# A macaron transformer block on one Trainium2 core: the low plane of the probabilities, made by GpSimd in its own slot or by VectorE one slot later

## The reference

```python
x = x + 0.5 * ffn(layernorm(x))      # gate, up: 256 -> 704, silu(gate)*up, down: 704 -> 256
x = x + attention(layernorm(x))      # causal, one head of width 256, 2048 keys a batch
x = x + 0.5 * ffn(layernorm(x))
```

```python
scores = Q @ K.T / sqrt(256); scores = where(causal, -inf, scores)
weights = softmax(scores);    out = weights @ V
```

## Time and profile before

| | |
|---|---|
| median of 3 runs | 1329.28 us |
| profiled execution, its own time | 1323.85 us |
| span of the profiled execution | 1322.0 us |
| PE busy | 1169.1 us (88%) |
| DVE busy | 1049.7 us (79%) |
| ACT busy | 732.5 us (55%) |
| POOL busy | 576.1 us (44%) |
| attention, as L549 runs | 473.8 to 920.0 us |

### The profile page before, as it was taken

One profiled execution on the slowest core, in us unless ns is written; L12 is line 12 of the kernel. 1 busy time (PEld: TensorE's weight loads), 2 busy tenths in 40 slices (PEclk: granted clock), 3 DMA queues, 4 the chain that ended last, 5 costly groups with the idle time before them and its releaser, 6 DMA issues.

```text
span 1322.0 us, 25381 instructions
## 1 busy us (share of the span) xinstructions
PE 1169.1 (88%) x7664; PEld 741.8 (56%) x7664; DVE 1049.7 (79%) x3443; ACT 732.5 (55%) x1475; POOL 576.1 (44%) x530
## 2 busy tenths in 40 slices
PE   0459999999998779998998999999999999999997
PEld 0226555555555456675666667566665555555554
DVE  4769999999999856546654764664799999999996
ACT  3556666666665435444543444465566666766653
POOL 1244445444544434443443444345344554454441
PEclk9879999999999989999999999999999999999998
DMA  9524434443443546664655566546355445444555
GB/s 317 116 54 81 88 74 86 78 89 72 88 78 71 106 81 101 120 115 94 108 102 105 97 116 119 98 79 125 63 97 105 102 100 107 103 105 98 109 105 115
DMA packets 462749, 134.46 MB, mean 102 GB/s; under 512 B 441296, under 2 KB 461904, under 8 KB 462672
## 3 DMA queue, kind: packets, MB, share of 16 engines
q1 hardware_dynamic: 454928, 125.62, 49.0%
q10 hardware_dynamic: 7744, 7.86, 1.9%
HBM read 11.34 MB, written 8.39 MB: 15 GB/s over the span
## 4 chain that ended last, share of the span: by engine, by line
DVE 31%; issue 26%; PE 25%; ACT 7%; POOL 7%; DMA 1%; SPq 1%; DVEq 1%; ACTq 1%; POOLq 0%
PE ps L1449 11%; PE ps L1437 8%; DVE arena L914 5%; DVE arena L974 4%; POOL arena L522 3%; DVE arena L918 3%; POOL arena L511 2%; DVE arena L1080 2%; DVE arena L903 2%; PE ps L1422 2%; ACT arena L645 2%; DVE arena L863 2%; PE ps L1402 2%; ACT arena L684 2%; PE ps L1415 2%
## 5 line engine op out<-in xcount | busy, mean ns | idle before, releaser
L1402 PE MATMUL ps<-wguT,arena 128*128 128x512 f16 (+1 forms) x2304 | 480.0, 363 | 28.7 <-DVE m_sb L1320 14.7
L1402 PEld LDWEIGHTS ps<-wguT,arena 128*128 128x128 f16 x2304 | 225.9, 98 | 250.6 <-issue 30.5
L522 POOL TENSOR_TENSOR arena<-arena 128x704 f32<-128x704 f32 x128 | 192.1, 1501 | 342.0 <-DVE arena L927 334.6
L1369 PE MATMUL ps<-wdT,arena 128*128 128x256 f16 x2176 | 264.2, 276 | 59.3 <-DMA arena<-arena 55.9
L1369 PEld LDWEIGHTS ps<-wdT,arena 128*128 128x128 f16 x2176 | 206.5, 99 | 124.5 <-issue 74.3
L549 POOL TENSOR_TENSOR arena<-arena 128x128 f16<-128x128 f32 (+7 forms) x64 | 143.8, 2247 | 236.6 <-ACT arena L745 197.7
L691 ACT ACTIVATE arena<-arena 128x704 int16<-128x704 f32 x128 | 100.9, 788 | 211.9 <-POOL arena L522 211.9
L1449 PE MATMUL ps<-arena 128*128 128x256 f16 x1632 | 188.9, 273 | 9.0 <-DVE x_sb L1096 8.9
L1437 PE MATMUL ps<-arena 128*128 128x512 f16 (+3 forms) x960 | 188.7, 349 | 3.5 <-ACT arena L745 3.5
L754 ACT ACTIVATE arena<-ps,arena,cst 128x128 f16<-128x128 f32 (+7 forms) x64 | 80.4, 1257 | 194.7 <-DVE arena L1085 190.7
L1449 PEld LDWEIGHTS ps<-arena 128*128 128x128 f16 x1632 | 158.3, 98 | 36.1 <-DVE x_sb L1096 7.2
(11 more groups left out here) (121 smaller groups left out, 1429.8 us busy)
## 6 DMA issues: line engine op xcount, KB each, us to landing
out_dram<-x_sb SPq DMA_DIRECT2D x32, 256.0 KB, 2.7
x_sb<-in_L_attn_x_dram ACTq DMA_DIRECT2D x3, 2048.0 KB, 17.8
arena<-arena SPq DMA_TRANSPOSE x384, 3.5
arena<-arena SPq DMA_DIRECT2D x8, 256.0 KB, 2.9
arena<-arena SPq DMA_DIRECT2D x4, 512.0 KB, 3.4
x_sb<-in_L_attn_x_dram ACTq DMA_DIRECT2D x1, 1536.0 KB, 7.4
arena<-in_L_ffn_w_down_dram SPq DMA_DIRECT2D x1, 704.0 KB, 8.4
arena<-in_L_ffn_w_gate_dram SPq DMA_DIRECT2D x1, 640.0 KB, 4.5
```

Source lines behind the costliest of these rows:

```text
L522: g.tensor_tensor(hy[u].rearrange("p (j b) -> p b j", j=BL), h[u].rearrange("p (b j) -> p b j", j=BL), hri[u].unsqueeze(2).to_broadcast([P ...
L1369: i = nc.tensor.matmul(ps_dn[w % 2], hT[w][:, c * P:(c + 1) * P], wdT[:, k, :], start=(s == 0), stop=(s == len(DOWN_STEPS) - 1))
L1402: i = nc.tensor.matmul(psf[:, 1536 * u + lo:1536 * u + hi], xv[:, u, xl, kt, :], wguT[:, wl, lo // P:hi // P, kt, :], start=(s == 0), stop ...
```

## The change

The function that makes the low plane is taken from GpSimd's program and put into VectorE's. Its waits, its operands and its semaphore stay the same. Its place does not: GpSimd made the low plane of tile s in slot s, VectorE makes that of tile s-1 in slot s, behind the softmax of tile s and ahead of the statistics, of z and of the add. Tile 15 of a batch is made in slot 16.

```diff
--- before.py
+++ after.py
@@ -539,20 +539,9 @@
                 nc.gpsimd.wait_ge(z_T, g * (32 * KT))
             nc.gpsimd.tensor_tensor(zq[1], zf, zq[0], ALU.subtract).then_inc(z_lo, 1)
 
-        def pool_p_lo(b, i):
-
-            k, w, q = i % 2, (i % TB + 1) * P, b * TB + i
-            nc.gpsimd.wait_ge(p_hi, q + 1)
-            nc.gpsimd.wait_ge(p_exp, q + 1)
-            if not isinstance(q, int) or q >= 2:
-                nc.gpsimd.wait_ge(pT_lo[color(i - 2)], landed(b, i - 2))
-            nc.gpsimd.tensor_tensor(pq[k][1][:, 0:w], prob[:, 0:w], pq[k][0][:, 0:w], ALU.subtract).then_inc(p_lo, 1)
-
         def pool_slot(b, s, last=False):
             if has_z(s, last) and s % GT == 1:
                 pool_z_lo(b * NG + (s // GT + 2))
-            if has_scores(s, last):
-                pool_p_lo(b, s)
             if has_z(s + 1, last) and s % GT == GT - 1:
                 pool_z_rstd(b * NG + ((s + 1) // GT + 2))
 
@@ -1095,6 +1084,15 @@
             xs = x_sb[:, bass.ds(col, D)]
             V.scalar_tensor_tensor(xs, ps_o, ofac, xs, ALU.mult, ALU.add).then_inc(o_add, 1)
 
+        def dve_p_lo(b, i):
+
+            k, w, q = i % 2, (i % TB + 1) * P, b * TB + i
+            V.wait_ge(p_hi, q + 1)
+            V.wait_ge(p_exp, q + 1)
+            if not isinstance(q, int) or q >= 2:
+                V.wait_ge(pT_lo[color(i - 2)], landed(b, i - 2))
+            V.tensor_tensor(pq[k][1][:, 0:w], prob[:, 0:w], pq[k][0][:, 0:w], ALU.subtract).then_inc(p_lo, 1)
+
         def dve_slot(b, s, last=False):
             g, q, t = b * NG + s // GT, b * TB + s, s - LAG
 
@@ -1110,6 +1108,8 @@
                 aux_lo_part()
             if has_scores(s, last):
                 dve_softmax(q, s, b * NCHUNK + chunks_before(s))
+            if s >= 1 and has_scores(s - 1, last):
+                dve_p_lo(b, s - 1)
             if not aux_first(s):
                 add_part()
                 aux_lo_part()
```

## The result

The changed kernel takes 1344.37 us, the median of 6 runs (1344.23 to 1351.39), beside 1327.76 us for the kernel before in 6 runs (1322.27 to 1331.13): a ratio of 1.0138, 95% interval 1.0107 to 1.017. (The ratios here are taken over all the runs; the quotient of the two medians is 1.0125.) It is slower by 16.6 us, as predicted in direction and inside the range. The forecast was 1342 and the sum behind it 13.0 us. The profiled execution took 1344.25 us, with a span of 1342.5 against 1322.0.

A forecast was written before the change was run, and what follows sets the result against it. TensorE's waits were taken to bound the program, no engine needing to be filled. Terms 2.6 + 3.2 + 5.1 + 2.1 = 13.0 us on 1323.85 gave 1336.9, and 1342 for the median, which ran 5.4 higher; range 1333 to 1351.

The forecast's parts named there:

- What is removed is worth nothing: GpSimd loses 64 subtractions, 143.8 us of work; value nothing, because nobody waited for what ended late.
- Batch 0: First batch: z transposes for slot 4 1.5 us late, covering slots 3 and 4 but for 0.1; slot 7 adds 0.99: 2.6 us.
- A pass: Loop pass, slots 3 to 8: 0.6 us from slots 3 and 4 plus 0.99 at slot 7, 1.6 us, twice.
- The ends: Slots 15 and 16 at three batch ends: TensorE waits for late z transposes, 1.7 us each, 5.1 us in all.
- (b): Batch end, SyncE's queue: z transposes issue behind tile 14's late low plane; 1.2 to 2.3 us, taken as 1.7.
- (a): Batch end, VectorE's queue: 1920 columns ahead of statistics and add make TensorE's weighted values 0.7 us late.
- The last batch: Slots 3 and 4 cost 0.6 us; in slot 11, 1408 columns delay softmax and exp of tile 12 by 1.53: 2.1 us.
- Contention: GpSimd's low plane of z beside VectorE's subtractions, sharing SBUF interfaces; expected done earlier in slots 5 and 9, nothing added.
- SyncE's queue backs up: Rival: tile 5's high plane lands late, ScalarE's exp for tile 7 waits 2.5 us, four times: 1352 us; chance 0.08.
- Packed mode: Rival: VectorE's subtraction runs at half the duration, total loss 6.5 us, 1336 us; chance 0.04.
- faster: Rival: GpSimd's slowness was on the path, 11.6 us come back if added pieces find cover, 1318 us; chance 0.04.
- no change: Rival: VectorE, idle 46 of 110 us, absorbs every piece and adds stay in time, 1329 us; chance 0.08.

The follow-up runs named there:

- covered pieces: Kernel before, with VectorE making 27 of 64 low planes (tiles 4, 5, 7 to 13, first three batches), GpSimd the others: 1330.58 us, ratio 1.0023.
- three pieces: Kernel before, with only the low planes of tiles 2, 3 and 6 of every batch made by VectorE: 1334.0 us, ratio 1.0059.
- z ahead: Kernel after, with z transposes issued ahead of the preceding tile's low plane in SyncE's queue (tiles 0, 4, 8, 14): 1341.59 us, ratio 1.0099.
- reciprocal later: Kernel after, with VectorE's reciprocal moved behind its small 32-column product in slots 9, 11 and 13 of the last batch: 1341.42 us, ratio 1.0118.
- late low plane: Kernel before, with SyncE transposing each low plane only once ScalarE has made the next tile's high plane: 1341.05 us, ratio 1.0103.
- last batch on GpSimd: Kernel after, with the last batch's low planes from tile 3 on made by GpSimd in their own slot: 1339.42 us, ratio 1.0099.

## Why the prediction was right, and where its sizes were off

- **What bounds the kernel**: right. TensorE had to be delayed only where it already waited, and the program took the delay over one to one. The covered pieces (39 us of VectorE's work, no lasting growth of the shift from slot 4 to slot 18) and the three pieces show it from both sides.
- **What is removed is worth nothing**: right, with one thing missed. GpSimd, no longer busy with its subtraction, came to its product of the last batch earlier and beside a VectorE operation, which cost 0.74 us twice on the path.
- **The duration of the subtraction**: right, 2147 ns for 1920 columns against 2.16 us; 1.01 us on the queue for 896 columns against 0.99.
- **Batch 0**: the z step was right, 1.5 us in the wait and 1.6 in the shift. The 0.6 of slots 3 and 4 was not covered by it: 1.6 us behind it instead of 1.1.
- **A pass**: 2.0 us in the undisturbed third pass against 1.6. What was mis-sized is the piece of slot 4: I took its 0.59 as covered by VectorE's idle 1.11 us, but in slot 4 itself z and the add stand behind it, and TensorE's wait for the add of slot 4 went from 0.25 to 0.94 us. The sum shows itself earlier than I had said: 0.6 at slot 4, 0.7 at slot 5, 0.4 at slots 6 and 7, and 0.3 at slot 8, so the wait at slot 8 is 1.19 and not 2 to 2.5 us. With the bound of 1.05 for slots 3 and 4 the sum would have been 2.04, near the measured 2.0, but the shift doesn't grow in those portions: slots 5 and 6, which I had taken as covered, show in it too, and slot 7 adds only 0.3 to a TensorE that is already late. A pass is 4.0 us longer than before (119.9 against 115.9, tile 5 to tile 5), not 3.3.
- **The ends**: the mechanism was right, the size too small, 2.3 us against 1.7, at the upper bound. The subtraction ended when I had said (698.24, less the shift of 8.88: 689.36), but z went out 1.66 us behind the low plane instead of 1.3, and TensorE got it at 706.95 - 8.88 = 698.07, the late end of my landings. That (b) decides and doesn't add to (a) was right: 0.94 and 2.5 us alone, 2.3 together. With z in time only the add's 0.94 is left (0.7 in the working), as the kernel with z ahead shows.
- **The last batch**: the step that failed. I followed the chain through the softmax and the exp of tile 12 and took 1.53 + 0.6. But TensorE waits in front of the weighted values of slots 10 and 12 for the adds of slots 9 and 11, which in VectorE's queue stand behind both the subtraction and the preparation: 1.80 and 2.34 us where there was no wait. The whole batch costs 3.9 us instead of 2.1, and 3.4 of it went away when GpSimd made these planes: 1.2 up to slot 7, where I had 0.6, and 2.7 behind it, where I had 1.5. Of the 2.7, about 1.3 are the meetings with GpSimd (next item), by the kernel with the reciprocal later. The exp of tile 12 made nobody wait any more, since TensorE was already later than that.
- **Contention**: "I add nothing, and no row shows the contention" was too quick. The Trainium skill (GPSIMD Engine Reference, Specifications) says that they contend when VectorE has two SBUF inputs; here it is measured at 0.74 us for each of two meetings, though not at the place at which I had looked for it. Two meetings of 0.74 are most of what the last batch cost above the forecast.
- **SyncE's queue backs up** (the rival at 1352): not in the loop. ScalarE's first exp waits for a DMA twice instead of once in attention, 8.3 us instead of 3.9; the new one, 3.0 us, is that of tile 7 in the last batch, with a wait of 0.51 us for z beside it. It is the sign that I had named for slot 7, seen in one of four batches; TensorE starts 0.7 us later there and has it back one tile later. **Packed mode**, **faster** and **no change** are ruled out by the durations and by the interval of the ratio.
- **The total**: nearer than its parts. The forecast for the median, 1342, stands on a median of three runs before, 1329.28; with the six it is 1327.76, and the same sum would have given 1340.8. The closeness of 1342 to 1344.37 is to that extent luck.

What stays open is the loop's turn. From tile 15 of a batch to tile 0 of the next, TensorE needs 11.2 to 14.0 us in the traces where the loop starts again (before: 11.4 and 12.2; after: 13.2 and 12.0; three pieces: 11.2 and 11.4; covered pieces: 13.3 and 13.7; late low plane: 13.9 and 14.0). The third time, where the last batch is written out behind the loop, the same 80 matmuls take 9.15 or 9.16 us in every one of the 14 traces, with no wait of TensorE above 0.2 us. So the 2 to 5 us above that, and their spread, go with starting the loop again. TensorE waits there 1.8 to 3.1 us, for "issue" or for VectorE's low part of the aux product, and VectorE is up to 1.8 us late in its first operation. The spread does not follow VectorE's loop body: the four kernels that have that of the kernel after (itself, z ahead, last batch on GpSimd, reciprocal later) need 13.2 and 12.0, 13.2 and 13.8, 13.2 and 13.4, 13.3 and 11.8 us. What sets it, the runs don't tell; it means that a difference of some 2 us between two traces in the ledger's row for the turn can't be put down to a change. The Trainium skill (Runtime: NRT & Kernel Launch, Instruction fetch mechanics) warns that a taken branch whose target is not among the instructions held forces a fetch; no run here isolates it.

## What to carry to other kernels

An engine with 40% idle time can still have no room at a given place. Ask of each place where work is put in what stands behind it in that queue and whether someone already waits for it; if so, the price is near the full duration, and if not, it is nothing. Ask too what else waits for the result: behind the add, the same operation had the next exp waiting for it and cost 20 us more. Do this for every copy of a stage by itself: the last batch, which had other work in the same queue, cost twice an ordinary pass. And an engine that is relieved starts its other work earlier, perhaps beside one that it disturbs.
